# A new order for the four hand-written instruction lists of a macaron transformer kernel

## The reference, cut to what matters

```python
x = x + 0.5 * ffn(layernorm(x), w_up, w_down)          # first outer FFN
x = x + attention_stack(layernorm(x), ...)             # 8 layers
x = x + 0.5 * ffn(layernorm(x), w_up, w_down)          # last outer FFN

# one layer of attention_stack
Q = elu(x @ Wq + bq) + 1;  K = elu(x @ Wk + bk) + 1;  value = x @ Wv + bv
KV = sum_s(K * value);     Ksum = sum_s(K)              # per sequence and feature
V = Q * KV / (Q * Ksum + 1e-6)
x = ln(gelu(V @ Wo + bo) + x)
x = ln(gelu(gelu(x @ W1 + b1) @ W2 + b2) + x)           # 128 -> 512 -> 128

# ffn: ternary weights, an RMS norm ahead of each product, exact gelu between
```

## Time and profile before

| | |
|---|---|
| runs | median 893.63 us (893.29 to 893.81, 3 runs) |
| span of the profiled execution | 892.1 us, 14583 instructions |
| TensorE busy | 849.9 us (95%); weight loads 587.8 us beside it |
| VectorE busy | 833.4 us (93%) |
| ScalarE busy | 798.2 us (89%) |
| GpSimd busy | 444.1 us (50%) |
| HBM read, written | 9.03 MB, 2.10 MB |

### The profile page before, as it was taken

The page is one execution under the profiler, slowest core; times in us unless marked ns, Lnnn a source line. Parts: engine busy times, 40 slices in busy tenths (PEclk is TensorE's granted clock), DMA queues, the critical chain, the costliest instruction groups (busy, mean ns, idle before and its releaser), DMA issues. The chain is left out here.

```text
span 892.1 us, 14583 instructions
## 1 busy us (share of the span) xinstructions
PE 849.9 (95%) x3915; PEld 587.8 (66%) x3915; DVE 833.4 (93%) x3349; ACT 798.2 (89%) x1136; POOL 444.1 (50%) x561
## 2 busy tenths in 40 slices
PE   4898789999999999999999999999999999998897
PEld 3797456666666666666666666666666666655787
DVE  6898778999999999999999999999999999989874
ACT  5876799999999999999999999999999999964883
POOL 4634235555555555555555555555555544435341
PEclk9998799999999999999999999999999999999999
DMA  5100000000000000000000000000000000000011
GB/s 167 28 2 1 0 9 1 1 16 13 9 1 16 14 9 7 9 17 6 13 4 16 6 15 2 22 1 15 1 13 1 1 0 1 1 1 1 13 37 48
DMA packets 19520, 12.06 MB, mean 14 GB/s; under 512 B 1160, under 2 KB 18288, under 8 KB 19440
## 3 DMA queue, kind: packets, MB, share of 16 engines
q1 hardware_dynamic: 19440, 11.13, 4.3%
HBM read 9.03 MB, written 2.10 MB: 12 GB/s over the span
## 5 line engine op out<-in xcount | busy, mean ns | idle before, releaser
L2039 POOL TENSOR_TENSOR x_lo<-x_fm,x_hi 128x512 fp32r<-128x512 f32 x120 | 153.8, 1282 | 231.0 <-DVE x_hi L1526 231.0
L488 PE MATMUL bank<-h,w 128*128 128x512 f32 x512 | 255.6, 592 | 0.0
L1290 DVE TENSOR_SCALAR z<-bank,mv,rstd 128x128 f32<-128x128 f32 x512 | 173.8, 403 | 6.5 <-POOL rstd L2031 3.8
L973 ACT ACTIVATE h<-bank,par 128x512 f32<-128x512 f32 x256 | 170.0, 691 | 8.5 <-PE bank L395 7.2
L393 PE MATMUL bank<-x_hi,w_hi 128*128 128x512 f32 x256 | 159.0, 621 | 0.3
L2031 POOL TENSOR_TENSOR rstd<-ve,minus_half 128x4 f32<-128x4 f32 x128 | 133.9, 1046 | 12.0
L393 PE MATMUL bank<-x_hi,wqkv_hi 128*128 128x512 f32 x192 | 108.1, 563 | 5.1 <-DVE phi_k L1420 4.2
L1276 DVE BATCH_NORM_STATS2 st<-bank 128x6 f32<-128x128 f32 x512 | 110.1, 281 | 2.8 <-PE bank L387 2.7
L488 PEld LDWEIGHTS bank<-h,w 128*128 128x128 f32 x512 | 91.0, 189 | 31.2 <-issue 18.7
L394 PE MATMUL bank<-x_lo,w_hi 128*128 128x512 f32 x256 | 100.9, 394 | 0.0
L395 PE MATMUL bank<-x_hi,w_lo 128*128 128x512 f32 x256 | 100.9, 394 | 0.0
(11 more groups left out here) (103 smaller groups left out, 1790.2 us busy)
## 6 DMA issues: line engine op xcount, KB each, us to landing
x_tm<-in_x SPq DMA_DIRECT2D x8, 256.0 KB, 3.7
raw_w<-in_W SPq DMA_DIRECT2D x8, 256.0 KB, 2.7
w<-in_W SPq DMA_DIRECT2D x8, 256.0 KB, 2.8
out<-x_tm SPq DMA_DIRECT2D x8, 256.0 KB, 2.3
raw_qkv<-in_Wk SPq DMA_DIRECT2D x8, 64.0 KB, 1.9
raw_qkv<-in_Wq SPq DMA_DIRECT2D x8, 64.0 KB, 2.0
raw_qkv<-in_Wv SPq DMA_DIRECT2D x8, 64.0 KB, 2.0
wo<-in_Wo SPq DMA_DIRECT2D x8, 64.0 KB, 2.5
```

The lines of the kernel that those rows point to most:

```text
L488: mm = pe.matmul(m.ps_o[:, :], m.w2[T.weights][:, c, :], m.h[:, T.par, c, :], start=c == 0, stop=c == FC - 1)
L973: act.activation(m.h[:, T.par, c, :], m.ps_h[c % 2][:, :], ACT.Gelu_apprx_tanh, bias=column(m, B1, T.layer, c, FC)).then_inc(s.gelu_h[T.pa ...
L1290: last = dve.tensor_scalar(dst[:, j, :], src(j), mv[:, j, 0:1], scale[:, j:j + 1], ALU.subtract, ALU.mult)
L2039: pool.tensor_tensor(m.x_lo[:, T.slot, :], m.x_fm[:, T.slot, :], m.x_hi[:, T.slot, :].bitcast(F32), ALU.subtract).then_inc(done, 1)
```

## The change

Every list is written anew. On TensorE, ScalarE and VectorE the calls are the same, each as often as before. Nothing else of the kernel is touched: buffers, banks, semaphores, SP's list and the work ahead of tick 2 stay.

- The steady tick starts at another point of the cycle (the opening ends, and the closing begins, a little earlier), and calls change places within it. `tiles_of` gets a lower bound, since a list may now name a job below 0.
- In the opening, the LayerNorm into the stack and the first layer's jobs (`turn_c`, `enter_full`, `enter_hi`, `project`) stand among the FFN work of slots 4 to 7; before, they stood behind it.
- In the closing, the calls of the last FFN and of the last layer are mixed differently, and `recip(Tile(63))` stands alone between gelus.
- On GpSimd, `split_next_qkv` and `split_next_w1` stand one or two ticks later.
- Counted from the lists, ScalarE's table loads go from 126 to 128: opening 12 to 9, each tick 4 as before, closing 2 to 7.

```diff
     def l(k, lag):
         job = 2 * (tick - lag) + k
-        return Tile(job, tick < OPENING + 3) if job < JOBS else None
+        return Tile(job, tick < OPENING + 3) if 0 <= job < JOBS else None
...
 # tensor_tick, opening
         outer_up(Outer(fin, 4), 2)
-        outer_up(Outer(fin, 4), 3)
         squares(Outer(fin, 3))
         outer_down(Outer(fin, 3), 0)
+        outer_down(Outer(fin, 3), 1)
+        outer_up(Outer(fin, 4), 3)
+        turn_c(Outer(fin, 0))
+        turn(pe, m, Outer(fin, 6), left)
         outer_up(Outer(fin, 5), 0)
...
+        project(Tile(0), KEY)
         outer_up(Outer(fin, 6), 2)
         outer_up(Outer(fin, 6), 3)
...
+        project(Tile(0), QUERY)
         outer_down(Outer(fin, 7), 0)
-        turn_c(Outer(fin, 2))
+        turn_c(Outer(fin, 4))
         outer_down(Outer(fin, 7), 1)
-        turn_c(Outer(fin, 3))
-        project(Tile(0), KEY)
-        project(Tile(0), QUERY)
+        project(Tile(1), QUERY)
+        project(Tile(1), KEY)
         project(Tile(0), VALUE)
...
 # scalar_tick, opening
         gelu(Outer(fin, 5), 0)
+        enter_full(Outer(fin, 0))
         gelu(Outer(fin, 5), 1)
-        normal(act, m, Outer(fin, 7))
         z_hi(act, m, Outer(fin, 6))
         gelu(Outer(fin, 5), 2)
         gelu(Outer(fin, 5), 3)
+        enter_hi(Outer(fin, 0))
         square(Outer(fin, 5))
...
 # gpsimd_tick, opening
+        split_next_qkv(Tile(2))
+        rms(Outer(fin, 0))
...
-        split_next_qkv(Tile(2))
-        split_next_qkv(Tile(3))
-        split_next_qkv(Tile(4))
...
 # vector_tick, closing
         residual(Tile(63), 1)
-        full(Tile(62), 1)
+        z_lo(dve, m, Outer(fout, 0))
+        var_eps(dve, m, Outer(fout, 3))
         stats(Tile(63), 1)
         means(Tile(63), 1)
-        z_lo(dve, m, Outer(fout, 0))
         x_in(Outer(fout, 5))
```

More of the change, by code:

```diff
@@ L685, in tensor_tick @@
         project(Tile(7), QUERY)
+        project(Tile(6), VALUE)
+        down(Tile(1), 3)
         project(Tile(7), KEY)
@@ L1247, in scalar_tick @@
     else:
+        exp(l(1, 0))
+        gelu_h(l(0, 2), 3)
+        gelu_o(l(1, 1))
+        gelu_h(l(1, 2), 0)
+        gelu_ff(l(0, 2))
+        gelu_h(l(1, 2), 1)
+        gelu_h(l(1, 2), 2)
+        full(l(0, 1), 0)
+        gelu_h(l(1, 2), 3)
+        log_den(l(0, 0))
+        negative(l(0, -1), KEY)
         negative(l(0, -1), QUERY)
@@ L1713, in vector_tick @@
-        attend(Tile(0))
-        neg_ksum(Tile(1))
-        over_ksum(Tile(1))
-        phi_q(Tile(1))
-        z_c(Outer(fin, 7))
-        sum_kv(Tile(1))
+        round_kq(Tile(2))
         sum_value(Tile(1))
-        mean_v(Tile(1))
-        round_kq(Tile(2))
         phi_k(Tile(2))
         phi_q(Tile(2))
+        neg_ksum(Tile(1))
+        mean_v(Tile(0))
+        neg_ksum(Tile(2))
+        over_ksum(Tile(1))
+        mean_v(Tile(1))
+        attend(Tile(0))
+        sum_kv(Tile(2))
+        over_ksum(Tile(2))
@@ L1754, in vector_tick @@
         attend(Tile(3))
-        sum_value(Tile(4))
-        mean_v(Tile(4))
+        residual(Tile(2), 0)
         hi(Tile(1), 0)
-        residual(Tile(2), 0)
+        over_ksum(Tile(4))
         stats(Tile(2), 0)
@@ L1797, in vector_tick @@
         z(Tile(60), 0)
-        residual(Tile(61), 0)
-        phi_q(Tile(63))
         phi_k(Tile(63))
         residual(Tile(58), 1)
-        neg_ksum(Tile(63))
-        hi(Tile(60), 0)
-        sum_value(Tile(62))
-        full(Tile(57), 1)
-        sum_kv(Tile(63))
-        over_ksum(Tile(62))
-        mean_v(Tile(62))
+        residual(Tile(61), 0)
+        full(Tile(57), 1)
+        phi_q(Tile(63))
+        sum_kv(Tile(63))
+        stats(Tile(61), 0)
+        hi(Tile(60), 0)
+        mean_v(Tile(62))
+        means(Tile(61), 0)
+        neg_ksum(Tile(63))
+        sum_value(Tile(63))
         over_ksum(Tile(63))
-        sum_value(Tile(63))
-        stats(Tile(61), 0)
-        means(Tile(61), 0)
-        attend(Tile(62))
+        x_in(Outer(fout, 0))
         stats(Tile(58), 1)
         means(Tile(58), 1)
-        x_in(Outer(fout, 0))
+        mean_v(Tile(63))
+        attend(Tile(62))
         z(Tile(61), 0)
@@ L1881, in vector_tick @@
-        full(Tile(63), 1)
-        alpha(dve, m, Outer(fout, 2))
-        alpha(dve, m, Outer(fout, 3))
-        x_in(Outer(fout, 7))
-        add_squares(Outer(fout, 0))
-        outer_means(dve, m, Outer(fout, 4))
-        outer_stats(dve, m, Outer(fout, 6))
-        mean_square(Outer(fout, 0))
-        z_lo(dve, m, Outer(fout, 2))
-        var_eps(dve, m, Outer(fout, 4))
-        beta(Outer(fout, 0))
-        outer_residual(Outer(fout, 0))
+        outer_stats(dve, m, Outer(fout, 4))
+        add_squares(Outer(fout, 0))
@@ L1893, in vector_tick @@
+        full(Tile(63), 1)
+        outer_means(dve, m, Outer(fout, 4))
+        outer_stats(dve, m, Outer(fout, 5))
+        x_in(Outer(fout, 6))
+        mean_square(Outer(fout, 0))
+        var_eps(dve, m, Outer(fout, 4))
+        outer_means(dve, m, Outer(fout, 5))
+        z_lo(dve, m, Outer(fout, 2))
+        beta(Outer(fout, 0))
+        var_eps(dve, m, Outer(fout, 5))
+        outer_residual(Outer(fout, 0))
+        outer_stats(dve, m, Outer(fout, 6))
         add_squares(Outer(fout, 1))
```

723 lines of the change are left out of this document (351 added, 372 removed).

## The result

The changed kernel takes a median of 887.66 us (884.29 to 887.85, 4 runs); the kernel before, beside it, 893.72 (893.29 to 893.84, 4 runs): a ratio of 0.9919, 95% interval 0.9900 to 0.9937. The forecast was 878.3: a gain of 15.4 us, of which 6.1 came. The profiled spans are 885.9 and 892.1 us, 6.2 apart.

A forecast was written before the change was run, and what follows sets the result against it. VectorE and TensorE were both taken as full from 190 to 745 us, with VectorE waits in the tick. Opening 8.3 + tick 5.0 + closing 2.0 = 15.3 us off the 892.1 span: 876.8, forecast 878.3 as median; range 867 to 891.

The forecast's parts named there:

- the waits named in the earlier trace: Steady tick, VectorE: z waiting for the power and means behind stats, 0.18 + 0.07 = 0.25 us per tick lost.
- The gelu hold: Tick, ScalarE: gelu_h moves behind an exp between two table switches; TensorE's 5.0 us cover suffices, costed at 0.
- rival 2: Tick: hi(b,1) copy collides with a GpSimd subtraction, 1.1 us per tick, 27.5 us slower, 906; chance 0.07.
- Sum 9.5, an estimate: Opening, VectorE before round_kq(4): 9.5 of at most 15.8 us idle stays, so the call comes 6.3 us earlier.
- waits for GpSimd's roots: Opening, VectorE's remaining idle time: beta(4) 0.8 us for GpSimd's root, and beta(6) 0.9.
- the two terms left at nothing: Opening: slow TensorE clock (5.4 us better to 2 worse) and stretched VectorE instructions (3.5 better to 5 worse).
- So both waits go: 0.25 us: Tick: work between means and z outlasts GpSimd's 1.44 us; 0.2 of 0.25 us taken per tick, 5.0 us.
- a sign of being wrong: The prediction called itself wrong if the tick grows, or if tiles 1 to 4 don't follow an early first tile.
- the closing: End of the kernel: z_lo and two normal calls move forward, 1.48 us wait goes; 2.0 us gained.
- the stretch to job 8: Opening from round_kq(4) on, to 165 us: VectorE's idle 6.62 us falls to 2.0 left; -2.0 in the parts table.
- rival 1: Tick stays as it is because TensorE, not VectorE, sets it: 883.3 us; chance 0.18.
- rival 4: Opening's new order puts in as many waits as it removes, and the tick stays: 891 to 895; chance 0.05.

The follow-up runs named there:

- after_warm: Changed kernel plus 15 idle 128x128 matmuls of ones on TensorE ahead of its first products (the warm-up): 885.17 us, ratio 0.9901.
- The runs with PSUM: Changed kernel, jobs 16 to 47: round_kq replaced by an instruction reading 448 or 512 columns from a PSUM bank: 881.60 and 881.02 us.
- the light runs: Work cut in jobs 16 to 47: half of phi_q, before 891.33, changed 883.65 us; one query matmul, before 893.12; half of negative, changed 887.81.
- before_kq: Kernel before, with round_kq(l(1,0)) moved ahead of z(l(1,3),1) in VectorE's steady tick: 917.68 us, ratio 1.0261.
- tick_hi_warm: Changed kernel plus 15 idle matmuls, with hi(l(0,3),1) right behind residual(l(0,1),0) in VectorE's tick: 906.55 us, ratio 1.0143.
- tick_vec: Changed kernel; VectorE's tick has hi(l(0,3),1) ahead of residual(l(0,1),0) and round_kq(l(1,0)) ahead of means(l(0,1),0): 885.99 us, ratio 0.9903.
- after_light_dve: Changed kernel, phi_q computed for only the first of the tile's two sequences in jobs 16 to 47: 883.65 us.
- after_kq860: Changed kernel, round_kq kept in SBUF but on the first 860 of 1024 columns in jobs 16 to 47: 886.57 us.
- after_light_act: Changed kernel, both ScalarE negative calls do only the first of two sequences in jobs 16 to 47: 887.81 us.
- after_port: Changed kernel, round_kq replaced in jobs 16 to 47 by a 128x448 instruction reading the query's PSUM bank: 881.60 us.
- after_port512: Changed kernel, round_kq replaced in jobs 16 to 47 by a 128x512 instruction reading the query's PSUM bank: 881.02 us.
- opening_alone: Opening list of the changed kernel, ticks and closing of the kernel before: 889.54 us, ratio 0.9958.
- closing_alone: Opening and ticks of the kernel before, closing list of the changed kernel: 889.51 us, ratio 0.9947.
- tick_vec_warm: Changed kernel with VectorE's tick changed as in tick_vec, plus the 15 idle matmuls at the start: 883.71 us, ratio 0.9885.

## Why the prediction was off

Where it was right: VectorE's work counts in the tick, and the waits named in the earlier trace rows went. The gelu hold costs nothing (the pair of table loads takes 412.85 to 416.51, 3.67 us again, and TensorE has no wait for `h` in the ticks), and TensorE's idle time in the closing fell in spite of the five more table loads there. Every copy to `x_hi` in the tick takes 0.42 us at most: rival 2's copy came first by 0.10 us (401.12 against 401.22).

**The step that failed first**, in size: "Sum 9.5, an estimate. 15.8 - 9.5 = 6.3 us gained at that point." Measured: 18.4 of idle, nothing gained. Of the 8.9 us between, 3.5 are two waits in the half-clock start (1.08 at 19.87 and 2.38 at 25.03), which are not in the list; in `after_warm` the first is gone, the second is 0.43, and 2.6 of the 6.3 come back. Another 2.1 are waits for GpSimd's roots: five of `beta` and one of the reciprocal ahead of `normal`, 3.8 us in all, where two were forecast at 1.7. One such root on GpSimd:

```profile
69.87 1.92 POOL L2063 TENSOR_TENSOR scale<-scale,plus_half 128x4 f32<-128x4 f32 x1 [1.78 <-DVE scale L1548]
```

It takes 1.92 us, beside `add_squares` (69.71 to 70.92, then 70.95 to 71.64), where others take 1.01; the eight of this kind from 40 to 116 us have a mean of 1.29, before 1.01. About 1.6 are in `add_squares`, tile 0's statistics and `z`; the rest is small ones. Only the start was tested; the roots are read from the trace. With a full-clock start the opening brings `round_kq(4)` to 111.0 to 112.0 in nine profiles, 2.5 to 3.4 us earlier than before, so about half of the forecast gain is missing even then. Of the two terms left at nothing, VectorE's busy time came out 2.6 us better, which the added idle time used up, and the granted clock up to `round_kq(4)` rose from 0.71 to 0.88 (second window of the earlier trace rows and of the table above) without bringing that call forward.

**The second** step that failed, in mechanism: "Between `means` and its `z` lie 1.8 to 2 us of other work, more than GpSimd needs for the add and the power ... So both waits go: 0.25 us." The duration of the power was taken from a place without `round_kq` beside it. I had weighed the shared port for the copies in rival 2 and not for the instruction that the new list puts beside the power. The runs with PSUM show its price: 0.17 to 0.25 us per tick, the whole gain. The tick grew from 22.18 to 22.24, which the prediction itself had named as a sign of being wrong.

**Two too small**: the closing, 2.0 taken from bounds of 0 to 6.05, measured 4.6; and the stretch to job 8, 3.1 instead of 2.0. That the time still lies within the wide range of 867 to 891 is luck: these two gave 3.7 us more than was asked, while the opening and the ticks lost 12.8.

The measured 887.7 lies between rival 1 (883.3) and rival 4 (891 to 895). Rival 1 had the unchanged tick, for a reason that the light runs refute. Rival 4, given 0.05, had both: an opening that puts as many waits in as it takes out, and the unchanged tick; only the closing and the stretch to job 8, which it did not count, kept the time below it. Rival 2 did not occur in this kernel, but a move of one instruction brings it (`before_kq`, `tick_hi_warm`).

**The half-clock start** does not follow from the opening's list. Eight versions have the changed opening list without the warm-up. In the profiles of four (the changed kernel, `tick_vec`, `after_light_dve`, `after_kq860`) the first eight products of 512 columns start 0.42 us apart or more, with `round_kq(4)` at 114.4 to 114.7; in the other four (`after_light_act`, `after_port`, `after_port512`, `opening_alone`) the distance comes down to 0.30 or less within them, with `round_kq(4)` at 111.2 to 112.0. **What stays open** is what decides it from one execution to the next, and whether the kernel before can have it: none of its five profiles without the warm-up, `closing_alone` among them, does. The changed kernel's run at 884.29 beside three at 887.6 to 887.9 would fit a full-clock start, but no profile shows it. The other waits of the opening were not tested one by one.

## What to carry to other kernels

When a reordered list hides a wait behind other work, ask of that work which memory both its ends are in: a duration from the old trace holds only beside the old neighbours. Where two engines are nearly full, a removed wait is worth at most the distance to what holds the tick next, so price the next wait before counting the first. Two engines that pass each other by 0.01 to 0.1 us at a shared place are a cliff: a move of one instruction cost 24 us here.

## What the runs showed of the hardware

- A GpSimd power of 128x4 isn't held in its middle: with `round_kq` starting 0.10 us behind its start it takes 1.04 us and `round_kq` its usual 0.69; with 0.01 to 0.02 us it takes 1.60. Where `round_kq` covers its end, it ends 0.04 us behind `round_kq`, whether that began 0.9 us behind the power's start (1.61; 1.52 with 860 columns) or 0.7 (1.40). The Trainium skill's page SBUF — State Buffer, section SBUF: two separate sides, says that whoever starts first holds the shared ports for the whole instruction. The 128x512 subtraction agrees (`mean_v` at 1.28, the copy at 1.03); the power doesn't, and the measurement decides: it held nobody.
- The granted clock that a view gives for a stretch can read full while the products run at half. The changed kernel's window at its start:

```profile
13.00:24.00 11.00, 9.98 (x43) 8.16 (x44) 8.22 (x44) 5.84 (x9) 5.68 (x6) 1.00 0.44 121
```

  The column says 1.00 where 512 columns take 0.42 us. The first clock record of this trace begins at 22.4 us, and there the distance between the down products (128 columns) falls from 0.21 to 0.11 us: the records agree with the products, but the column counts time without a record as full. The Trainium skill's page TensorE: Matmul & The Clock Gate, section Seeing it yourself, warns that clock events in a profile have been observed to be unreliable; here what misleads is their absence. The distance between starts is the surer reading.
- An early full clock does not settle the clock later on. From 85 to 115 us, where TensorE has gaps, the granted clock is 0.78 in `after_warm` and 0.79 in `after_light_act`, but 0.94 in `opening_alone` and `tick_vec_warm`, all with the changed opening and a full-clock start; it is 0.88 in the changed kernel. `round_kq(4)` comes at 111.9 and 112.0 in the first two and at 111.2 and 111.5 in the other two.
